# Mixture-of-experts layer with top-capacity routing: second biases of all eight experts added by two wide products

## The reference, cut to what matters

```python
N = B * S                                   # 1024 tokens, D = 128, E = 8, F = 512
k = int(CAPACITY_FACTOR * N / E)            # 128 tokens for each expert
route_prob = softmax(xf @ Ws + bs, axis=-1).T
route_vals, routes = top_k(route_prob, k)   # each expert picks its 128 tokens
xin = xf[routes]
h = gelu(einsum('ekd,edf->ekf', xin, W1) + b1[:, None, :])
out = einsum('ekf,efd->ekd', h, W2) + b2[:, None, :]
out = out * route_vals[..., None]
final = zeros((N, D)).at[routes.reshape(-1)].add(out.reshape(-1, D))
```

## Time and profile before

| | us |
|---|---|
| median of 3 runs | 606.18 |
| lowest, highest | 605.25, 607.37 |
| profiled execution, first to last instruction | 618.7 |
| PE busy in it | 545.9 (88%) |
| DVE busy | 396.9 (64%) |
| ACT busy | 303.2 (49%) |
| POOL busy | 223.6 (36%) |

### The profile page before, as it was taken

The page is one execution under the profiler, slowest core; times in us unless marked ns, Lnnn a source line. Parts: engine busy times, 40 slices in busy tenths (PEclk is TensorE's granted clock), DMA queues, the critical chain, the costliest instruction groups (busy, mean ns, idle before and its releaser), DMA issues.

```text
span 618.7 us, 12164 instructions
## 1 busy us (share of the span) xinstructions
PE 545.9 (88%) x3982; PEld 426.4 (69%) x3982; DVE 396.9 (64%) x2193; ACT 303.2 (49%) x758; POOL 223.6 (36%) x227
## 2 busy tenths in 40 slices
PE   4889779997899899989999879888699899979997
PEld 2565337874667566768677657677477778979997
DVE  3565765534433598776598998956757898744543
ACT  2342314325775676674874646635574555322221
POOL 4016830002434464563553556541614334340000
PEclk9996889999999999998988999968889999999999
DMA  4500102404000000000000000003500000010000
GB/s 129 179 1 14 40 25 68 124 30 154 3 1 1 0 2 1 3 1 2 2 2 1 2 2 1 2 2 102 179 22 10 14 15 19 18 31 1 27 1 10
DMA packets 23050, 19.17 MB, mean 31 GB/s; under 512 B 2048, under 2 KB 18508, under 8 KB 22989
## 3 DMA queue, kind: packets, MB, share of 16 engines
q1 hardware_dynamic: 22477, 17.36, 9.2%
q0 software_dynamic: 512, 1.05, 0.6%
HBM read 15.38 MB, written 3.01 MB: 30 GB/s over the span
## 4 chain that ended last, share of the span: by engine, by line
PE 65%; DVE 20%; ACT 8%; issue 4%; another core or an unknown queue 1%; POOL 1%; DMA 0%; DVEq 0%; ACTq 0%
PE ps L1797 54%; DVE wk L1159 4%; PE ps L2187 4%; DVE top L1149 3%; DVE nmax L1101 2%; ACT w_mem L1549 2%; PE ps L2249 2%; ACT prT L1562 2%; DVE sel_mem L994 1%; PE ps L2382 1%; DVE xn L1122 1%; PE ps L2441 1%; PE ps L1809 1%; DVE xn L838 1%
## 5 line engine op out<-in xcount | busy, mean ns | idle before, releaser
L1101 DVE TENSOR_REDUCE nmax<-ps 128x2 f32<-128x256 f32 (+1 forms) x64 | 51.2, 821 | 63.9 <-PE ps L1797 62.0
L1159 DVE MATCH_REPLACE8 wk<-top,wk 128x77 f32<-128x77 f32 x384 | 80.5, 223 | 0.9 <-issue 0.9
L687 POOL TENSOR_TENSOR w_mem<-w_mem,rinv 128x256 f32<-128x256 f32 (+3 forms) x44 | 53.2, 1219 | 53.9 <-DVE rinv L1107 53.4
L1280 DVE TENSOR_TENSOR sel_mem<-gr,ps 128x512 f32<-128x512 f32 x47 | 32.2, 685 | 53.4 <-ACT gr L1739 52.7
L1149 DVE MAX8 top<-wk 128x8 f32<-128x77 f32 x384 | 58.2, 223 | 1.9 <-DVE top L1149 1.8
L1739 ACT ACTIVATE gr<-ps 128x512 f32<-128x512 f32 x47 | 28.1, 598 | 62.2 <-PE ps L1797 62.2
L1797 PE MATMUL ps<-cat_mem 64*128 64x512 f32 (+7 forms) x272 | 54.0, 477 | 1.5 <-ACT cat_mem L1533 1.5
L716 POOL TENSOR_SCALAR wk<-wk 128x616 f32<-128x616 f32 x16 | 28.1, 1755 | 60.6 <-DVEq L1163 60.3
L1549 ACT ACTIVATE w_mem<-ps,nmax 128x128 f32<-128x128 f32 (+3 forms) x88 | 44.4, 519 | 11.1 <-DVE nmax L1101 10.9
L1797 PE MATMUL ps<-prT,cat_mem 128*64 128x128 f32 x640 | 45.5, 293 | 1.4 <-DVE x L1184 0.9
L611 POOL TENSOR_TENSOR rstd<-var_eps,minus_half 128x4 f32<-128x4 f32 x8 | 8.2, 1025 | 97.8 <-DVE var_eps L831 97.7
(11 more groups left out here) (346 smaller groups left out, 1372.8 us busy)
## 6 DMA issues: line engine op xcount, KB each, us to landing
w_mem<-in_L_ffn_W_dram SPq DMA_DIRECT2D x12, 256.0 KB, 3.1
f_mem<-in_L_ffn_Wg_dram SPq DMA_DIRECT2D x8, 256.0 KB, 2.7
f_mem<-in_L_ffn_Wu_dram SPq DMA_DIRECT2D x8, 256.0 KB, 3.1
f_mem<-in_L_ffn_Wd_dram SPq DMA_DIRECT2D x8, 256.0 KB, 4.1
sel_mem<-in_L_ffn_W_dram SPq DMA_DIRECT2D x4, 256.0 KB, 4.8
xs_dram<-zero SPq DMA_DIRECT2D x1, 960.0 KB, 6.3
ys_dram<-f_mem SPq DMA_DIRECT2D x15, 64.0 KB, 1.5
xs<-xs_dram SPq DMA_DIRECT2D x3, 256.0 KB, 4.7
```

The source lines that it names most:

```text
L687: pool.tensor_tensor(pr[s][:, :, at:at + n], pr[s][:, :, at:at + n], rinv[:, i % 8, :].unsqueeze(2).to_broadcast([P, 2, n]), ALU.mult)\
L1101: dve.tensor_reduce(nmax[:, i % 8, :], ps[:, 2 * s:2 * s + 2, at:at + (c + 1) * P], X, ALU.max, negate=True).then_inc(nmax_ready, 1)
L1159: dve.match_replace(wk[q][:, t, h, :], top[q][:, t, h, 8 * r:8 * r + 8], src[:, t, h, :], GONE).then_inc(top_step, 1)
L1280: dve.tensor_tensor(hg[s][:, :], gr[s][:, :], ps[:, 2 * s + 1, :], ALU.mult)\
```

## The change

Each expert's one-row product is taken out, and the second-layer product's last instruction now ends the group and signals y_ps. In its place the biases of all experts are added to the scattered sum itself, in banks 6 and 7, by one product for each half of the batch: rows_b2 (8 experts x 128) with chosenT (8 experts x 512 tokens), where chosenT holds the expert's share if it chose the token, and 0 if not.

The parts:

- SyncE: b2 is loaded as 8 rows of 128, not as 1 row of 1024.
- VectorE: one more instruction after select(0, 0): slot_eq = (slot < 127.5) x prob, 128 x 64.
- TensorE, ahead of the first expert: eight transposes of slot_eq into banks 6 and 7, instead of four filling products; they wait for that instruction.
- ScalarE, in expert 0, after gathered(1) and before yhi: two copies of 8 x 512 from banks 6 and 7 to chosenT.
- TensorE, scatter(0): one more wait, for these copies, since its first product overwrites the banks.
- TensorE, expert 7: the two wide products, plain f32, in place of keep_busy(0, 6).

```diff
@@ -404,7 +404,8 @@
 
         cat_mem = sb_early("cat_mem", [P, (2 * NP + 1) * S])
 
-        row_b2 = cat_mem[0:1, 14 * S:14 * S + E * D]
+        rows_b2 = cat_mem[0:E, 14 * S:14 * S + D]
+        chosenT = cat_mem[0:E, 12 * S:14 * S]
         w_a0 = part(f_mem, 3 * S, 3, D)
         qT = cat_mem[:, 8 * S:10 * S]
         kT = cat_mem[:, 10 * S:12 * S]
@@ -527,8 +528,7 @@
             for k, w in enumerate((x0_wq, x0_wk, x0_wv)):
                 sp.dma_start(w_x0[:, k, :], w).then_inc(in_x0, 16)
             sp.dma_start(ctx_sb[:, :, :], ctx_in.rearrange("b n d -> n b d")).then_inc(in_x0, 16)
-            sp.dma_start(row_b2, f0_b2.rearrange("(a e) d -> a (e d)", a=1))\
-              .then_inc(in_b2, 16)
+            sp.dma_start(rows_b2, f0_b2).then_inc(in_b2, 16)
             sp.dma_start(ws[:, :], f0_ws).then_inc(in_x1, 16)
             for k, w in enumerate((x1_wq, x1_wk, x1_wv, x1_wo)):
                 sp.dma_start(w_x1[:, k, :], w).then_inc(in_x1, 16)
@@ -1071,6 +1071,8 @@
                                          ALU.mult, ALU.subtract).then_inc(y_ready, 1)
 
             select(0, 0)
+            dve.scalar_tensor_tensor(slot_eq[:, :, :], slot[:, :, :], CAP - 0.5, prob[:, :, :], ALU.is_lt, ALU.mult)\
+               .then_inc(chosen_ready, 1)
             select(1, 1)
             gate_of(0, 0)
             turn_sel(0, 0)
@@ -1519,6 +1521,10 @@
                                    bias=vec[:, VEC["b1"] + FC * e + c:VEC["b1"] + FC * e + c + 1]).then_inc(h_ready, 1)
                 if e + 1 < E:
                     gathered(e + 1, 1 - q)
+                if e == 0:
+                    for b in range(B):
+                        act.wait_ge(wide_ps, 2 * B + b + 1)
+                        act.activation(chosenT[:, b * S:(b + 1) * S], ps[0:E, 6 + b, :], ACT.Copy).then_inc(wide_ready, 1)
                 act.wait_ge(y_ps, e + 1)
                 act.wait_ge(gate_ready, e + 1)
                 if e >= 2:
@@ -2038,6 +2044,8 @@
             def scatter(e, q):
                 pe.wait_ge(selT_ready, B * (e + 1))
                 pe.wait_ge(y_ready, e + 1)
+                if e == 0:
+                    pe.wait_ge(wide_ready, 3 * B)
                 for b in range(B):
                     at = slice(b * S, (b + 1) * S)
                     mm(ps[:, 6 + b, :], yhi[:, q, :], selT[:, q, at], start=e == 0, stop=False, shared=True)
@@ -2082,14 +2090,14 @@
                     gather(e + 1, 1 - q)
                     spread(e + 1)
                 else:
-                    keep_busy(0, 6)
+                    for b in range(B):
+                        mm(ps[:, 6 + b, :], rows_b2, chosenT[:, b * S:(b + 1) * S], start=False, stop=False, shared=True)
                 pe.wait_ge(h_ready, FC * (e + 1))
                 if e:
                     pe.wait_ge(y_ready, e)
                 for c in range(FC):
-                    mm(ps[:, 5, 0:D], hid[q][:, c, :], w2[e % 3][:, c, :], start=c == 0, stop=False)
-                mm(ps[:, 5, 0:D], ones[0:1, :], row_b2[:, D * e:D * (e + 1)], start=False)\
-                    .then_inc(y_ps, 1)
+                    last = mm(ps[:, 5, 0:D], hid[q][:, c, :], w2[e % 3][:, c, :], start=c == 0, stop=c == FC - 1)
+                last.then_inc(y_ps, 1)
                 if e + 1 < E:
                     turn_rows(e + 1, 1 - q)
                 if e:
@@ -2105,7 +2113,11 @@
                 last = pe.transpose(ps[0:E, 2 + t // TB, t % TB * P:(t % TB + 1) * P], slot[:, t, :], ident[:, :])
                 if t % TB == TB - 1:
                     last.then_inc(wide_ps, 1)
-            keep_busy(4, 4)
+            pe.wait_ge(chosen_ready, 5)
+            for t in range(NT):
+                last = pe.transpose(ps[0:E, 6 + t // TB, t % TB * P:(t % TB + 1) * P], slot_eq[:, t, :], ident[:, :])
+                if t % TB == TB - 1:
+                    last.then_inc(wide_ps, 1)
             turn_rows(0, 0)
             pe.wait_ge(wide_ready, 2 * B)
             spread(0)
```

## The result

| | before | changed |
|---|---|---|
| median of the first comparison, 4 runs each | 605.71 us | 599.68 us |
| lowest, highest of it | 602.86, 607.37 | 598.20, 601.11 |
| ratio, 95% interval | | 0.9885 (0.985 to 0.9921) |
| span of the first trace | 618.7 us | 599.2 us |
| the experts, from share of expert 0 to the first x | 45.43 us | 42.29 us |

A forecast was written before the change was run, and what follows sets the result against it. TensorE was taken to bound the experts' stretch. Terms -4.2 (one-row products), +0.8 (copies) and +0.6 (wide products) sum to -2.8 us, from the median 606.18 to 603.4 us; range 601.7 to 605.5.

The forecast's parts named there:

- What bounds the kernel: In the first layer's experts TensorE is busy throughout, 5.20 of 5.20 us per expert; time taken from it comes off the end.
- The one-row products, 8 x 0.53: In each of eight experts, removing the one-row bias product saves 0.53 us: 4.2 us in all, bounds 3.3 to 4.6.
- The copies on ScalarE, +0.8: Expert 0: two copies before yhi delay selT, so TensorE stands still 0.8 us before expert 2's spreading; bounds 0.3 to 1.1.
- The wide products in expert 7, +0.6: Expert 7: two wide products replacing six fillers outlast the gelus' cover and lose 0.6 us; bounds 0.3 to 0.7.
- The pauses at 8 rows: Expert 7: changing rows costs the wide products 0.09 us at each end; without the pauses their term is 0.3, not 0.6.
- Transposes, the VectorE instruction, the load: Before the experts: eight transposes, one extra VectorE instruction and the bias load in eight pieces cost nothing; at most 0.1 us.
- I take the 2.8 off the median as it is: Whole kernel: the 2.8 us saved is subtracted from the runs' median of 606.18, giving 603.4 us.
- half a microsecond of scatter on either side: Range of the whole time: bounds 602.2 to 604.7 widened by this scatter and most of one clock fall, to 601.7 to 605.5.
- The rivals: No stall, 602.6 us, chance 0.11; pause stays, 605.8, 0.07; one clock fall, 605.1, 0.13; long clock fall, 608.5, 0.06.
- the clock falls once: One more fall of TensorE's clock, in the experts or later, costs up to 1.7 us: 605.1 us, chance 0.13.

The follow-up runs named there:

- r2_after: The changed kernel again, no edit, beside the kernel before: 602.54 us median of 6 runs, ratio 0.9913 (0.9884 to 0.9941); experts 42.29 us.

## Why the prediction was right or wrong

The stretches of the experts, in one table (each from the traces named above). The forecasts are put together from the terms of the prediction:

| kernel | experts, us | against before | by the prediction's terms |
|---|---|---|---|
| before | 45.43 | | |
| without the one-row products | 40.89 | -4.54 | -4.2 |
| one-row products made 128 rows | 42.67 | -2.76 | |
| changed | 42.29 | -3.14 | -2.8 |
| changed, without the wide products | 41.65 | -3.78 | -3.4 |
| changed, copies late | 41.48 | -3.95 | -3.6 |
| changed, copies late, no fillers before the last scattering | 40.87, 40.85 | -4.56, -4.58 | |
| changed, pushed back by 3.46 | 45.71 | +0.28 | |

- **What bounds the kernel.** Right: TensorE's own list bounds the stretch, and 0.57 taken from it eight times came off the end of the stretch.
- **The one-row products, 8 x 0.53.** The mechanism was right, the size measured is 0.57, at my upper bound: the turning's weights are loaded ahead, and its pair gains 0.07 by it where I had counted 0.03. What the one row adds, which I put at 0.09 a product from one pair of rows, is 0.35 by the run with 128 rows, since it also stretches the two instructions themselves (0.41 against 0.23) and the pair behind.
- **The copies on ScalarE, +0.8.** Right: 0.75 of idle in the trace, 0.80 won back when they stand behind yhi.
- **The wide products in expert 7, +0.6.** Right: 0.60 in the trace and 0.64 by the run without them. The pauses at 8 rows are there: the first wide instruction starts 0.98 after the start of the first-layer product, and the fillers started 0.89 after it, 0.09 earlier. The rule of the Trainium skill ("TensorEngine Tiling (Array Packing)", "Key Properties") that a change of the tiling mode drains TensorE agrees with these pauses on both sides of the sum; that they are such a drain, no run shows.
- **Transposes, the VectorE instruction, the load.** Right, nothing: the turning ahead of expert 0 is released as before. What the Trainium skill says of transposes and the clock ("TensorE: Matmul & The Clock Gate", "Part 4: PE-mode transpose") had no effect here; the granted clock was 1.00 through the experts of the changed kernel. The eight transposes take 0.9 us, so this says nothing of longer rows of them.
- **The step that failed: "I take the 2.8 off the median as it is", and the range with "half a microsecond of scatter on either side".** The median of three runs, 606.18, was a fair centre (the mean of 87 runs is 606.2), but each mean of four runs carries about 1.3 us of scatter (2.7 for a single run), since the clock's falls ahead of the experts and behind them move an execution by up to 10. The measured 599.68 lies 3 us under the mean of 28 runs of the same kernel, 602.6, which is 0.8 under the forecast and inside the range; the 24 later runs alone have 603.1. The four runs that the forecast was held against had a clock of 0.9785 instead of 0.972, which is worth 3.0 us. I had the means to see this: the profiled execution was 12.5 us over the median, with clock 0.91 in the second layer, and I put that down to the profiler. That the later mean lies so near the forecast is in part luck: the term of the one-row products was 0.3 too small in all, and the centre, a median of three runs, could have lain 1.5 us off.
- **The rivals.** None of the four occurred in the first trace of the changed kernel. In r2_after, one of its four traces, the clock fell for 3.4 us at 141.7, where the kernel before kept 1.00: there the rival "the clock falls once" is seen, in the stretch whose clock of 1.00 I had held against it. One fall more or less of the clock was the right idea in size, and wrong in kind: I gave it to the change, with a chance of its own, where it belongs to every single execution and should have widened every case's time.

What stays open: what decides in which executions the clock falls. The distance at equal clock, 3.1 with a standard error of 0.3, leaves no room for more than some tenths of a microsecond beside the experts' 3.14; whether the change moves the mean clock itself by as little as 0.001 can't be told. Nor is it known why the version without the four fillers has a lower mean clock.

## What to carry to other kernels

A product with one row of weights between products of 128 rows cost far more here than its columns: 0.57 us against 0.22 for a full one, so biases are better gathered into one product at a place where TensorE has room, or given all rows. A copy added to an engine that is idle for more than half the time still stalls the bound engine if it stands ahead of what that engine waits for; look for the idle behind it. And before a forecast is laid on a median, compare the traced execution's span with the runs: if it differs, read the granted clock by stretch, and take the scatter of single executions into the range. When the result is in, compare the mean clocks of the two sets of runs before the difference of their times is put down to the change.

## What the runs showed of the hardware

- An f32 product of one row and 128 columns between products of 128 rows took 0.57 us (45.43 - 40.89 = 4.54 over eight), one of 128 rows in its place 0.22 (42.67 - 40.89 = 1.78 over eight). The 0.35 lie in the steps into the one row, between its two instructions, and behind it.
- One program's executions on this chip, alone on one core, spread from 601.2 to 611.1 us, and go with the mean granted clock: at 0.979 and over the mean is 602.8, at 0.969 to 0.970 it is 606.6, by the line through all runs 4.5 us for 0.01.
- A wait of ScalarE 2.7 us longer than its like, with no sender in the record, stands in one of 14 traces, and the end of that execution came 2.7 us later by it.
